# First layer: the routed experts' silu products, made for all tokens without their weights and weighted at the down projections

## What is computed

```python
x = x + 0.5 * _L0_ffn_ref(_layernorm(x), ...)          # block 1, and again block 3

def _L0_ffn_ref(x, ...):                                # 7 routed experts, 1 shared, top 2, capacity T // 7 = 292
    shared_sum = ffn(x, shared_w1, shared_w2)           # ffn: h = x @ w1; x1, x2 = split(h); x1 * silu(x2) @ w2
    aff = sigmoid(x @ gate_w + expert_bias)
    mask = the two largest of aff for each token
    score = where(mask, aff, -1).T
    _, sel_idx = top_k(score, capacity)                 # for each expert, its 292 best tokens
    w = where(kept, aff, 0)                             # weight of a kept token, 0 for the others
    out = vmap(_ffn)(x[sel_idx], routed_w1, routed_w2)
    return shared_sum + zeros.at[sel_idx].add(out * w)
```

## Time and profile before

| | us |
|---|---|
| median of 3 runs | 3719.99 (3718.23 to 3720.12) |
| the profiled execution | 3711.44 |
| its span, first to last instruction | 3709.6 |
| busy in the span: PE, DVE, ACT, POOL | 3038.5, 2194.1, 1489.1, 1115.9 |
| mean granted TensorE clock, share of full speed | 0.895 |

### The profile page before, as it was taken

The page is one execution under the profiler, slowest core; times in us unless marked ns, Lnnn a source line. Parts: engine busy times, 40 slices in busy tenths (PEclk is TensorE's granted clock), DMA queues, the critical chain, the costliest instruction groups (busy, mean ns, idle before and its releaser), DMA issues.

```text
span 3709.6 us, 56721 instructions
## 1 busy us (share of the span) xinstructions
PE 3038.5 (82%) x19164; PEld 2581.3 (70%) x19164; DVE 2194.1 (59%) x5486; ACT 1489.1 (40%) x3661; POOL 1115.9 (30%) x1085
## 2 busy tenths in 40 slices
PE   4597999999999955889479796948888685986698
PEld 2476888888888834769458594836666574975597
DVE  3644555555555546556473667657778667655664
ACT  2124443444444321233532344437677344424342
POOL 2002222222222220054350544541111455431543
PEclk8798999999999967999779997859899887998899
DMA  2002111111111110033110243520000263311232
GB/s 77 1 0 92 64 48 63 47 63 47 65 45 66 47 46 0 7 95 111 46 34 0 88 124 94 135 74 2 1 1 1 70 160 115 105 56 46 85 107 74
DMA packets 115095, 222.71 MB, mean 60 GB/s; under 512 B 17313, under 2 KB 66945, under 8 KB 110273
## 3 DMA queue, kind: packets, MB, share of 16 engines
q1 hardware_dynamic: 80754, 149.30, 12.5%
q0 software_dynamic: 21472, 58.36, 6.1%
q10 hardware_dynamic: 12672, 12.58, 1.0%
HBM read 172.74 MB, written 47.85 MB: 59 GB/s over the span
## 4 chain that ended last, share of the span: by engine, by line
PE 37%; issue 29%; DVE 16%; POOL 8%; ACT 5%; DMA 4%; SPq 0%; DVEq 0%; ACTq 0%; POOLq 0%
PE bank L502 9%; PE bank L504 9%; PE bank L503 9%; POOL HWL L1737 3%; POOL YG L1498 2%; POOL KL L1753 2%; PE bank L1081 2%; PE bank L1997 1%; DVE ST L528 1%; PE bank L2013 1%; ACT XN L552 1%; PE bank L1103 1%; DMA YG<-dyo,POSI 1%; DMA MXG<-dxn,IDX 1%; DVE SG L749 1%
## 5 line engine op out<-in xcount | busy, mean ns | idle before, releaser
L1488 POOL DMA_INDIRECT MXG<-dxn,IDX x250 | 237.5, 950 | 319.2 <-PE bank L1081 163.8
L1753 POOL TENSOR_TENSOR QL<-QG,QH 128x512 fp32r<-128x512 f32 x64 | 83.0, 1296 | 729.7 <-ACT QH L1645 729.7
L1498 POOL DMA_INDIRECT YG<-dyo,POSI x192 | 190.1, 990 | 218.2 <-DMA dyo<-YS 110.7
L1683 DVE TENSOR_TENSOR X<-bank,X 128x512 f32<-128x512 f32 x128 | 82.5, 686 | 226.9 <-PE bank L504 226.9
L622 PE MATMUL bank<-TAB,XN 128*128 128x128 f32 x320 | 72.8, 385 | 168.1 <-ACT XN L552 127.7
L1480 POOL TENSOR_TENSOR MWL<-RAW,MWH 128x608 fp32r<-128x608 f32 (+2 forms) x118 | 182.1, 1553 | 79.2 <-ACT MWH L1184 73.0
L1478 POOL CAST MWH<-RAW 128x608 fp32r<-128x608 f32 (+2 forms) x78 | 55.0, 705 | 467.6 <-DVE X L884 369.1
L622 PEld LDWEIGHTS bank<-TAB,XN 128*128 128x128 f32 x320 | 52.2, 196 | 181.7 <-ACT XN L552 114.3
L502 PE MATMUL bank<-MWH,GH 128*128 x500 | 173.9, 348 | 0.0
L2174 DVE COPY PT<-bank 128x384 f32<-128x384 f32 x256 | 131.8, 551 | 64.0 <-PE bank L1997 55.3
L502 PE MATMUL bank<-MWH,SHH 128*128 128x256 f32 x352 | 110.1, 313 | 72.2 <-DVE SHL L1357 57.9
(11 more groups left out here) (439 smaller groups left out, 11201.2 us busy)
## 6 DMA issues: line engine op xcount, KB each, us to landing
dyo<-YS SPq DMA_DIRECT2D x250, 128.0 KB
RAW<-in_wheads SPq DMA_DIRECT2D x68, 320.0 KB, 3.0
RAW<-in_eL SPq DMA_DIRECT2D x64, 304.0 KB, 2.9
BB<-dgates SPq DMA_DIRECT2D x17, 1024.0 KB, 4.5
GB<-dgates SPq DMA_DIRECT2D x17, 1024.0 KB, 6.5
dxn<-XN ACTq DMA_DIRECT2D x16, 512.0 KB, 4.3
RAW<-in_eL SPq DMA_DIRECT2D x32, 256.0 KB, 2.7
RAW<-in_sL SPq DMA_DIRECT2D x18, 384.0 KB, 3.9
```

The lines of the kernel that those rows point to most:

```text
L1488: nc.gpsimd.indirect_dma_start(MXG[:, n % XGS, :], None, dxn, bass.IndirectOffsetOnAxis(ap=IDX[:, b:b + 1], axis=0)).then_inc(x_in[n % XGS ...
L1498: nc.gpsimd.indirect_dma_start(YG[:, i % YGS, :], None, dyo[0:m.blocks * P, :], bass.IndirectOffsetOnAxis(ap=POSI[:, c * NT + t:c * NT + t ...
L1753: nc.gpsimd.tensor_tensor(lo[:, :], src[:, :], f32(hi[:, :]), ALU.subtract).then_inc(qk_ready, 1)
```

## The change

The block gets functions of its own (`l0_tensor`, `l0_scalar`, `l0_vector`), and what the stage AFT needs of the old rounds stays as `aft_*`.

- The router's logits are made as in the later layers: in `front_tensor`, pair of tiles by pair (four matmuls with 32 rows out, one copy LGS, two small matmuls), with 8 warming matmuls on constants after each pair's transposes.
- Scores are repeated 16 times by two copies on VectorE (SCW, 128 x 896 each), turned on TensorE to 112 rows, and copied to SC half by half. The eight DMAs through `dscore` are gone.
- The up steps of the routed experts no longer wait for the weights: product silu x up, unweighted, goes to HID, a tile of 128 x 7 x 2048 in SBUF. Two stand in each of the 8 search steps, four between search and weights, eight among the first down steps.
- The count of a search step stands on TensorE behind two up steps. VectorE works on products and the shared expert between flags and count.
- The kept weights are made token by token in the layout 128 x 7 x 16 (`keep0_flags`, `keep0_weights`: 3 and 11 operations over some 112 elements, a memset, and two matmul steps for the ranks of equal scores), turned on TensorE in 16 small transposes and copied to CT, 32 rows, a high and a low part.
- A down step i is: comb(i), product HID x weights to HF (`weighted`), HH, HL, down(i). TensorE's order is up (as long as any is left), down(i), comb(i+2). Windows 2 and 3 add into banks 0 to 3 in place of 6 and 7.

The core of the diff:

```diff
-            SG = r.put('SG', [112, T])
+        SG = r.put('SG', [112, T], BF16)
+        HID = r.put('HID', [P, L0_E, T])
+        SEARCH = len(SHIFTS)
+        WINDOW_BANKS = (6, 6, 0, 2)
+        def expert_of(x):
+            return x // L0_E, 1 + x % L0_E
+        def l0_tensor(pe, st):
+            front_tensor(pe, st)
+            def up(s):
+                w, j = (s, 0) if s < NW else expert_of(s - NW)
+                if s >= 2:
+                    pe.wait_ge(h_done, st.steps + s - 1)
+                up_tensor(pe, st, j, s % 2, w * W).then_inc(up_done, 1)
...
+            def comb(i):
+                w, j = expert_of(i)
+                if i == 0:
+                    pe.wait_ge(l0_copied, 8 * (st.l0 + 1))
+                if i >= 2:
+                    pe.wait_ge(prod_done, EXPERTS * st.l0 + i - 1)
+                nc.tensor.matmul(bank[4 + i % 2][:, :], HOTS[:, j - 1, :], CT[:, w * W:(w + 1) * W],
+                                 start=True, stop=True).then_inc(comb_on, 1)
+            def down(i):
+                w, j = expert_of(i)
+                if i == 0:
+                    pe.wait_ge(shared_done, NW * (st.l0 + 1))
+                elif j == 1 and WINDOW_BANKS[w] == WINDOW_BANKS[w - 1]:
+                    pe.wait_ge(x_done, st.xd + w)
+                elif j == 1:
+                    pe.wait_ge(h_done, st.steps + NW + EXPERTS)
+                pe.wait_ge(h_ready, st.steps + NW + i + 1)
+                down_tensor(st, j, i % 2, j == 1, j == L0_E, WINDOW_BANKS[w])
+            up(0)
+            up(1)
+            scores0_tensor(pe, st, 0)
+            up(2)
+            scores0_tensor(pe, st, 1)
+            up(3)
+            for n in range(SEARCH):
+                if n < NW:
+                    shared_out(n)
+                up(NW + 2 * n)
+                up(NW + 2 * n + 1)
+                count0_tensor(pe, st, n)
+            up(EARLY_UPS)
+            least0_tensor(pe, st)
+            up(EARLY_UPS + 1)
+            ranks0_tensor(pe, st)
+            up(EARLY_UPS + 2)
+            up(EARLY_UPS + 3)
+            kept0_tensor(pe, st, 0)
+            kept0_tensor(pe, st, 1)
+            comb(0)
+            comb(1)
+            for i in range(EXPERTS):
+                if 1 <= i and EARLY_UPS + 3 + i < NW + EXPERTS:
+                    up(EARLY_UPS + 3 + i)
+                down(i)
+                if i + 2 < EXPERTS:
+                    comb(i + 2)
...
+        def l0_vector(dve, st):
...
+            product(0)
+            product(1)
+            scores0_kept(dve, st, 0, 1)
+            shared_low(0)
+            scores0_kept(dve, st, 1, 1)
+            shared_low(1)
+            for n in range(SEARCH):
+                search0_flags(dve, st, n)
+                if n == 0:
+                    product(2)
+                product(NW - 1 + 2 * n)
+                product(NW + 2 * n)
+                if 1 <= n < 3:
+                    shared_low(n + 1)
+                if n < NW:
+                    shared_in(n)
+                search0_least(dve, st, n)
+            product(EARLY_UPS - 1)
+            keep0_flags(dve, st)
+            product(EARLY_UPS)
+            keep0_weights(dve, st)
+            product(EARLY_UPS + 1)
+            kept0_kept(dve, st, 0, 1)
+            kept0_kept(dve, st, 1, 1)
+            dve.wait_ge(shared_done, NW * (st.l0 + 1))
+            for i in range(EXPERTS + 1):
+                if i < EXPERTS:
+                    weighted(i)
+                if i:
+                    low(i - 1)
+                if EARLY_UPS + 2 + i < NW + EXPERTS:
+                    product(EARLY_UPS + 2 + i)
+                if i >= 2 and (i - 1) % L0_E == 0:
+                    window_in((i - 1) // L0_E - 1)
+            window_in(NW - 1)
```

More of the change, by code:

```diff
@@ L107, in __init__ @@
         self.tailed, self.next = tailed, None
-        (self.pieces, self.steps, self.prods, self.ln, self.tr, self.l0, self.moe, self.added, self.blocks, self.xd, self.gates) = before
+        self.routed = kind == 'moe' or name == 'L0'
+        self.router = self.m.router if self.m else 0
+        (self.pieces, self.steps, self.ln, self.tr, self.l0, self.moe, self.rt, self.added, self.blocks, self.xd, self.gates) = before
 FFNS = {
-    'L0': Layer(J=L0_E + 1, comb=(1, L0_E + 1), E=8, act=ACT.Silu, gated=True, scale=0.5),
-    'AFT': Layer(J=L1_DFF // P, comb=(0, 0), E=0, act=ACT.Silu, gated=True, scale=1.0),
+    'L0': Layer(J=L0_E + 1, act=ACT.Silu, scale=0.5),
+    'AFT': Layer(J=L1_DFF // P, act=ACT.Silu, scale=1.0),
 }
@@ L174, in build @@
         ORD = main.put('ORD', [P, 16])
-        PARTS = main.put('PARTS', [112, 2])
+        HALR = main.put('HALR', [32, 16], F32R)
         ST6 = main.put('ST6', [P, NT, 6])
@@ L444, in build @@
         stages = []
-        pieces = steps = prods = ln = tr = l0 = moe = added = blocks = xd = gates = 0
+        pieces = steps = ln = tr = l0 = moe = rt = added = blocks = xd = gates = 0
         for s in STAGES:
@@ L520, in banks_of @@
         def banks_of(st):
[L521 removed]
+            return TURN_BANKS if st.routed else RING
         def front_moments(dve, st, g):
@@ L804, in down_tensor, with round_tensor @@
             last.then_inc(down_done, 1)
[L806 removed]
+        def round_tensor(pe, st, i):
             ff = st.f
[L810 to L834 removed]
@@ L836, in last_down @@
-        def last_down(pe, st, j0, count):
+            before = at(nc.tensor, i, ff.J, st.steps)
+            for j in range(ff.J):
+                up_tensor(pe, st, j, j % 2, at(nc.tensor, i, W, 0)).then_inc(up_done, 1)
+                if j:
+                    pe.wait_ge(h_ready, before + j)
+                    down_tensor(st, j - 1, (j - 1) % 2, j == 1, False)
+                elif not isinstance(i, int):
+                    last_down(pe, st, before)
+        def last_down(pe, st, count):
@@ L2617, in ffn_weights @@
         return np.ascontiguousarray(np.concatenate(parts, axis=2))
-    def selector(rows, width, expert_of):
-        s = np.zeros((rows, width), np.float32)
-        for u in range(width):
-            for row in expert_of(u):
-                s[row, u] = 1.0
-        return s
     a = {k: np.asarray(v) for k, v in a.items()}
```

507 lines of the change are left out of this document (241 added, 266 removed).

## The result

The changed kernel took 3679.98 us in the median of four runs (3663.8 to 3690.78), the kernel before beside it 3720.05 (3718.23 to 3733.22). The ratio is 0.9882, with a 95% interval of 0.9856 to 0.9909: 44 us less by the ratio. In a later group of runs the same pair gave 0.9906 (0.9869 to 0.9944). The profiled execution took 3684.48 us, 27 us less than that of before. The number lies in the predicted range, but by luck: what made it isn't what was predicted.

What follows compares the result with a forecast made beforehand. Bounds: an engine-to-engine chain in the search, VectorE while weights are made, TensorE in the rounds. Blocks save 61.1 us less 9 for restarts: 3711.44 - 52 = 3659.4; runs stand 8.55 higher, so 3668 us, range 3642 to 3694.

Steps and rivals of the forecast that it cites:

- restarts: TensorE's new rests in each block cost time at the low clock: 1.5 + 2 + 1 = 4.5 us a block.
- the tail at the low clock: From down(9) on, TensorE's rests bring its clock down: 25 us a block more, 3718 us for both blocks; chance 0.13.
- a PEclk of 1.0 in that tail: Sign expected in the trace: TensorE at its high clock through the last down steps, 3.4 us each.
- Router: From the last rows normalised to the router's result: 14.27 us instead of 15.12, a gain of 0.85.
- First candidate: Start of the search: first candidate 14.4 us after the router's result instead of 22.4, with 1.0 us for a copy to SCW.
- Search step: Each of eight search steps, set by the chain between engines: 7.6 us against 3.93 before, with routed up steps done inside.
- that rival: In the search, a cheaper flags pass because SG is bfloat16: 5 us a block less, 3658 us; chance 0.05.
- the slower case: The search runs at the low clock: 97 us instead of 61, 36 us a block more, 3740 us; chance 0.04.
- Weights: Between search and rounds: weights ready (CT) in 15.5 us instead of 24, with four more up steps done in it.
- Steps 1 to 8: Down steps 1 to 8, each with an up step before it: 4.48 us each, 35.8 us together.
- The stall: At down(7), which waits for window 0's addition because it uses the same banks: 2.75 us.
- The tail's step at the high clock: Down steps 9 to 27, chain of comb, weighted, low part and down: 3.38 us each, between 3.2 and 4.0.

Runs made afterwards that it cites:

- kernel with fillers: Eight matmuls of 256 columns on constants added before each down step of the tail, against the changed kernel; ratio 0.9848 to the kernel before, or 3663 us.
- kernels with the comb ahead: comb(i+2) put before down(i) on TensorE, against the changed kernel: ratio 0.9697 to the kernel before, or 3607 us; further variants were built on it.

## Why the prediction was right in its number, by luck, and wrong in its reason

*Forecast and rivals.* I gave 3668 us with 61 us from the blocks less 9 for restarts. Measured were 3680, and the blocks of the first profile gave 2.4 us, those of the second, against both profiles of before, 8 to 10. The rival that I gave 0.13, the tail at the low clock, is what happened, in both blocks of every profile of this order. Its own time for that, 3718, was missed by 38 us, because stages that neither case contained got faster. That the number fell into the range is luck: the 52 us of the two blocks didn't come, and 22 us by the profiles, 36 by the medians, came from outside the blocks and the start.

*The step that failed* is the clock of the tail: "a PEclk of 1.0 in that tail". I let two stretches with loosely spaced matmuls at 1.00 outweigh the one row at 1288.47 and the stretch at 0.50. The kernel with fillers shows the price: 22.5 and 21.6 us a block, near the rival's 25. The Trainium skill, TensorE: Matmul & The Clock Gate, section "A second HAM failure mode: psum-queue depth-cycling", has a kernel with short rests between groups of matmuls whose clock falls and comes back again and again. The trace agrees: in the first profile's block 1 the clock is back from 242 to 248 and from 269 to 275 us, and low for most of the rest of the tail.

*Term by term, block 1, from the router's result.*
- Router: 0.85 us gained was forecast. From the first row statistics it takes 36.59 us against 35.49 before in block 1, and 37.62 against 38.08 in block 3: nothing either way.
- First candidate: 13.2 us, forecast 14.4. A copy to SCW is 0.58 us, not 1.0. That is no rule for a broadcast source: the copy to HOTS, 896 elements from a broadcast too, takes 1.07 us.
- Search step: 9.97 us for the first, 7.37 to 7.77 for the next three with a shared down step, 7.17 without; forecast 7.6 for all. The end of the search is at 74.6, forecast 77.9. The flags pass is 2.35 us with a bfloat16 output too: that rival falls. The 1227 ns in the perf-mode tier table of the Trainium skill's VectorE: DVE Perf Modes don't hold for this form, as before the change.
- The search at the high clock: right, a mean of 1.00 from 64 to 125 us in block 1 and from 1347 to 1408 in block 3, so the slower case had no ground.
- Weights: the first comb 16.2 us after the search, forecast 15.5 and a little.
- Steps 1 to 8: 4.85 us, forecast 4.48. I took comb and down from the kernel before, where the comb follows an up step without a wait, at 1.66 us; it is 1.94 here. 3 us a block.
- The stall: 2.61 us, forecast 2.75.
- The tail's step at the high clock: 3.50 us, forecast 3.38, bounds 3.2 to 4.0. The sum to the tail's start was 3.8 us short at comb(10) (140.8 against 137.0); from there to the end it took 88.2 us against 63.8. Of these 24.4 some 21 are the 14 steps that ran wholly or mostly at 0.50, 1.53 us each.
- The dropped loads "cost nothing that I can see": the first row statistics start 2.6 us earlier in the first profile, and 1.5 to 2.8 in the ten others without either load. Which load does it isn't shown; one of them, put back, made 1 us at most.

*What stays open.* From the end of block 3 on the profiles of the changed kernel and of its variants on chips like the first (before at 3713 to 3720 us) took 2119.7, 2131.8, 2118.9 and 2132.5 us, those of before 2140.9 and 2149.8. Most of it is attn2, 451.8 to 466.6 against 469.9 and 479.7. Its code is the same; the stops of VectorE shown above account for some 17 us of it. What ends them, and why the changed kernel hasn't them, isn't shown. The trace has one lead. The DMA queue that carries instructions (q14) moves 37 packets of 8 KB in attn2 in before and in the changed kernel, and 12 or 13 in the kernels with the comb ahead; in these the stop ahead of the copy to PT, 1.8 to 2.1 us above, is gone as well. So the stops seem to go with the loading of code, and the change alters how much of VectorE's code stands ahead of attn2's. But with the same 37 loads the changed kernel has one stop where before has two. A run that changes nothing but the code's length would test it. What else moves this stage's clock, 457.5 and 495.6 us in two executions of the changed kernel on different chips, isn't settled either.

So of the 44 us some 5 to 13 are the blocks' and the start's and some 17 lie in the five stretches of attn2, an effect of the change that nobody forecast; the rest isn't explained.

## What to carry to other kernels

Work that is moved out of a loop takes its cover with it: write down the chain of the steps that are left, and if a result made one step ahead would break it, move that matmul ahead first (here one line's place, 40 to 50 us a block). Where a forecast leaves TensorE a rest in every step, take the low clock as the case to be ruled out, and price the stretch at both levels. And add up the profile by stages before calling a prediction right: here the total agreed and the blocks didn't, and a third or more of the gain lay in a stage that the change doesn't touch.

## What the runs showed of the hardware

- TensorE with 1.38 us of rest in every 3.50 us fell to a granted clock of 0.50 and stayed there for 19 us and for over 40 us at a time, with brief returns; with the same chain and eight small matmuls in each rest it held 1.00 for 62 us.
- At 0.50 the rest was 1.38 us as well, and TensorE was busy 14.38 of 20 us: the step grew from 3.50 to 5.03 us and the rest didn't shrink.
- A 512-column matmul in float32r between two instructions that wait takes 0.42 us to the next start, in bfloat16 0.32; both have a gap of 0.21 us ahead, where matmuls of one group start 0.12 us apart.
- An accumulating VectorE pass over 2048 float32 elements takes 2.35 us, with a float32 or a bfloat16 output. Two copies of 896 elements, both from a broadcast source, take 0.58 and 1.07 us.
- The same code, in a stage that wasn't touched, ran with one stop of VectorE more at five places (1.31 to 1.61 us each) in one kernel and without it in twelve profiles of others. The five stretches together took 113 us in the one and 96 in the first of the others.
- The kernel before differed by 2% between groups of runs, 3713 to 3795 us. The stages with routed experts show it (the fourth stage 211 to 215 us in the profiles of the faster groups, 217 to 226 in the others); the attention behind block 1 took 1016.6 to 1019.5 us in all of them.
